# Graph attention kernel: VectorE adds the last step of a chunk in the next turn, behind the next chunk's scores, first messages and first product

## What is computed

```
Q = (h @ Wq).reshape(n, H, HD)
K = (h @ Wk).reshape(n, H, HD)
V = (h @ Wv).reshape(n, H, HD)
score = jnp.einsum('ehd,ehd->eh', K[src], Q[dst]) / np.sqrt(HD) + edge_bias
m = jax.ops.segment_max(score, dst, num_segments=n)
ex = jnp.exp(score - m[dst])
denom = jax.ops.segment_sum(ex, dst, num_segments=n)
attn = ex / denom[dst]
out = jax.ops.segment_sum(attn[:, :, None] * V[src], dst, num_segments=n)
```

## Time and profile before

| | us |
|---|---|
| median of 3 runs | 5411.74 |
| lowest and highest run | 5407.52, 5449.04 |
| span of the profiled execution | 5404.7 |
| first and last add of the pass (L785) | 309.2, 1864.1 |
| DVE busy over the whole span | 3064.0 (57%) |
| PE busy over the whole span | 3933.5 (73%) |

### The profile page before, as it was taken

The page is one execution under the profiler, slowest core; times in us unless marked ns, Lnnn a source line. Parts: engine busy times, 40 slices in busy tenths (PEclk is TensorE's granted clock), DMA queues, the critical chain, the costliest instruction groups (busy, mean ns, idle before and its releaser), DMA issues. The chain is left out here.

```text
span 5404.7 us, 69347 instructions
## 1 busy us (share of the span) xinstructions
PE 3933.5 (73%) x16281; PEld 2847.1 (53%) x16282; DVE 3064.0 (57%) x7623; ACT 1859.8 (34%) x5073; POOL 2464.9 (46%) x2442
## 2 busy tenths in 40 slices
PE   6867777777777659967853666666666338999999
PEld 4545555555555448856732444444444226777776
DVE  3278887878888766662154666666667773111111
ACT  1333333333333312311222444444444322333332
POOL 2256665656666450001166666666663422333332
PEclk8988988888888879977986788777887559999999
DMA  2555555555555232211173333333331451111111
GB/s 80 186 146 149 154 151 148 151 140 153 147 148 151 83 118 84 91 55 40 52 252 89 95 96 96 94 95 94 93 96 47 127 194 20 32 32 31 31 31 27
DMA packets 316127, 553.64 MB, mean 102 GB/s; under 512 B 63431, under 2 KB 213783, under 8 KB 315857
## 3 DMA queue, kind: packets, MB, share of 16 engines
q0 software_dynamic: 137120, 388.63, 27.4%
q1 hardware_dynamic: 178736, 161.98, 9.8%
HBM read 459.75 MB, written 90.62 MB: 102 GB/s over the span
## 5 line engine op out<-in xcount | busy, mean ns | idle before, releaser
L427 POOL DMA_INDIRECT attend_ring<-kv_rows,all_step_src x880 | 860.1, 977 | 624.5 <-PE attend_ps_agg L468 371.3
L931 POOL DMA_INDIRECT edge_ring<-head_rows,all_step_src x880 | 878.7, 999 | 457.1 <-issue 204.2
L967 PE MATMUL edge_ps_agg<-edge_msg,edge_sel 128*128 128x264 f32 x1760 | 676.3, 520 | 188.9 <-issue 57.3
L468 PE MATMUL attend_ps_agg<-attend_msg,attend_sel 128*128 128x264 f32 x1760 | 605.1, 445 | 179.7 <-DVE graph_qa L785 122.9
L967 PEld LDWEIGHTS edge_ps_agg<-edge_msg,edge_sel 128*128 128x128 f32 x1760 | 414.5, 257 | 328.2 <-issue 198.7
L1266 DVE TENSOR_TENSOR graph_acc<-graph_acc,edge_ps_agg 128x264 f32 x880 | 369.9, 420 | 367.2 <-PE edge_ps_agg L967 169.0
L2821 DVE TENSOR_TENSOR moe_gl<-moe_ps_h,moe_act 128x341 f32<-128x341 f32 x210 | 107.8, 514 | 776.8 <-PE moe_ps_h L2739 776.8
L452 PE MATMUL attend_ps_q<-graph_qa,attend_sel_t 128*128 x1760 | 527.7, 429 | 27.4 <-ACT attend_sel_t L581 17.8
L785 DVE SCALAR_TENSOR_TENSOR graph_qa<-graph_qa,all_step_same,attend_ps_agg 128x264 f32 x880 | 421.1, 479 | 170.1 <-remote 121.0
L468 PEld LDWEIGHTS attend_ps_agg<-attend_msg,attend_sel 128*128 128x128 f32 x1760 | 329.3, 208 | 347.2 <-issue 148.6
L2739 PE MATMUL moe_ps_h<-experts_w,moe_xt 128*128 x1680 | 501.7, 451 | 0.6 <-ACT moe_xt L2770 0.6
(11 more groups left out here) (424 smaller groups left out, 6587.9 us busy)
## 6 DMA issues: line engine op xcount, KB each, us to landing
attend_ring<-kv_rows,all_step_src POOLq DMA_INDIRECT x880
edge_ring<-head_rows,all_step_src POOLq DMA_INDIRECT x880
kv_rows<-qkv_kv SPq DMA_DIRECT2D x25, 512.0 KB, 2.9
experts_w<-in_w_t SPq DMA_DIRECT2D x16, 682.0 KB
attend_mask<-run_starts SPq DMA_DIRECT2D x440, 8.1 KB
edge_mask<-run_starts SPq DMA_DIRECT2D x440, 8.1 KB
head_rows<-hds_hh SPq DMA_DIRECT2D x25, 264.0 KB
qkv_x<-in_x SPq DMA_DIRECT2D x25, 256.0 KB, 3.3
```

What stands on the lines that cost most here:

```text
L427: nc.gpsimd.indirect_dma_start(ring[:, step % RING1, :], None, g.kv_rows, bass.IndirectOffsetOnAxis(g.step_src[:, step:step + 1], 0)).then ...
L468: nc.tensor.matmul(ps_agg[i % SUM_BANKS][:, 0:AGG], sel[:, q % 2, u % QU, :], msg[:, q % 2, u % QU, :], start=True, stop=True).then_inc(s_ ...
L931: nc.gpsimd.indirect_dma_start(ring[:, n % slots, u, :], None, g.head_rows, bass.IndirectOffsetOnAxis(g.step_src[:, step:step + 1], 0)).th ...
L967: nc.tensor.matmul(ps_agg[i % BANKS][:, 0:AGG], sel[:, q % 2, u % QU, :], msg[:, q % 2, u % QU, :], start=True, stop=True).then_inc(s_agg, 1)
```

## The change

The adds of a chunk's steps 0 to 14 stay where they are. The add of step 15 leaves the end of its turn. It now stands in the next turn behind score_of(a), messages(b, 0) and product(c, 0), and ahead of the load of the first eight block numbers (rows_of), which moves behind it with it. The rows of the last turn are handed on from turn to turn as last. Behind the last turn one add is left. No instruction is added or taken away.

```diff
-            def turn(c, a, b):
-                at = rows_of(b, 0) if b is not None else [None] * U
+            def turn(c, a, b, last):
                 of(a, score_of)
                 of(b, messages, 0)
                 of(c, product, 0)
+                if last is not None:
+                    add(b - 1, last, CH - 1)
+                at = rows_of(b, 0) if b is not None else [None] * U
                 of(a, tails_of)
                 of(c, product, 1)
                 of(a, heads_of)
...
                 of(b, add, at, 12)
                 of(b, add, at, 13)
                 of(c, dot, 3)
-                of(b, add, at, 14, 15)
-
-            turn(0, None, None)
-            turn(1, 0, None)
+                of(b, add, at, 14)
+                return at if b is not None else None
+
+            last = turn(0, None, None, None)
+            last = turn(1, 0, None, last)
             for i in range(1, count - 1):
-                turn(i + 1, i, i - 1)
-            turn(None, count - 1, count - 2)
-            turn(None, None, count - 1)
+                last = turn(i + 1, i, i - 1, last)
+            last = turn(None, count - 1, count - 2, last)
+            last = turn(None, None, count - 1, last)
+            add(count - 1, last, CH - 1)
             v.wait_ge(s_add, count * CH)
```

## The result

The changed kernel takes 5491.68 us (median of 4 runs, 5483.99 to 5497.41), the kernel before 5423.92 us beside it (4 runs, 5407.52 to 5449.04). The ratio is 1.0135, with a 95% interval of 1.0111 to 1.0158: 1.35% slower, clear of noise. The prediction's direction was wrong. The prediction said 5407 us, in a range of 5370 to 5438. The profiled execution of after has a span of 5482.0 us, 77.3 more than before.

The account below looks back on a forecast made before the run. A chain of hand-overs, with add-up 15's late signal, then ACT and PE, was taken to set the turn. Span 5404.7 less 5 gave 5399.7; plus 7.0 to the runs' median, 5407 us, range 5370 to 5438.

Parts of the forecast that it names:

- (a): At the turn's end, DVE's score, messages and product fill idle time ahead of add 15, cutting it from 121 to 47 us.
- (c): After add 15, DVE could start scan L700 0.75 us behind it and reach copy L710 about 1.4 us earlier.
- the wait at L710: DVE's wait at copy L710 for PE's row product was to grow from 50.7 to some 125 us.
- (d): Queue behind copy L710 gains nothing: PE waits for ACT, ACT for add-up 15's signal, which hangs on PE alone.
- R2: Rival: add-up 15's signal comes earlier because PE's transpose is queued sooner; all of it 121 us, 5291 us; chance 0.04.
- (e): New waits: add 15 ends up to 1.1 us later where its signal is prompt, hidden by ACT's 2.2 us.
- (f): At copy L710, 14 turns where DVE is late gain 0.33 us each, 5 us in all.
- R3: Rival: PE's clock drops behind the idle stretch after add-up 15, 1.57 us per turn, 83 us, 5495 us; chance 0.07.
- The sign that it named: For the clock loss on PE: the granted clock of the first graph's pass falls below 0.88.
- R1: Rival: DVE's lead counts in full, each turn 1.4 us shorter, 74 us, 5338 us; chance 0.08.

Follow-up runs that it names:

- e5: Changed kernel with ACT's first denominators of the next chunk ahead of its wait for add-up 15: 0.9993 of before (5414.85 us), again 0.9977 (5409.26 us), on late chips.
- e1: Changed kernel with DVE's score back behind add 15, first messages and product still ahead: 1.0034 of before on a calm chip, repeats 1.0040, 1.0042 and 1.0031.
- e2: Changed kernel with only the score ahead of add 15, first messages and product behind it again: 1.0043 of before on a calm chip, repeats 1.0037 and 1.0033.
- e6: Kernel before with ACT's first denominators of the next chunk ahead of its wait for add-up 15: 1.0062 of before, 5451.85 us, on a late chip.
- e7: Changed kernel with PE's transpose of the scores issued six times instead of once: 1.0138 of before on a late chip.
- e8: Changed kernel with PE's transpose issued six times and add-up 2 of each chunk four times: 1.0169 of before on a late chip.
- e9: Changed kernel with first-pass gathers cut to 64 of 512 values per row, ring zeroed first, for timing only: 5075.44 us, 1.009 of before, on a calm chip.

## Why the prediction was wrong, step by step

- (a) held as to the work: DVE does it from 1062.29 to 1063.77, in idle time. It did not hold as to the idle time. 116.9 us are left, 47 were expected: the signal moved away by nearly as much as was filled.
- (c) and the wait at L710 held: 119.3 us, some 125 expected. On a calm chip 39.8 became 95.6.
- (d) failed. Its sentence was "G itself hangs on PE alone". The engine that makes the signal did nothing later, and still the signal came 1.15 us later on average, 3.06 instead of 1.91 behind the shown end; that is two thirds of the 1.74 us that a turn lost. The rest of (d), that DVE's lead leads nowhere because the copy waits for PE and PE for ACT, held: PE's first add-up kept its 2.16 us behind ACT, and when e5 takes ACT away, messages that are there early let it start 4.7 us sooner, for 1.5 us of the turn. The prediction noted that it did not know what holds the signal, and priced that only in the direction of a gain (R2).
- (d) was also short of a term: PE reaches its waits for DVE earlier and works at a lower clock behind them. Between the copy and the carries that is 0.27 of the 0.37 us that a turn loses on a calm chip. Over the pass the adds run over 1422.1 us there, against 1406.8 in before, 15 of the 22 us by which the medians differ.
- (e) held as to what follows ACT: PE's first add-up started 2.16 us behind it, 2.17 before.
- (f), the gain of 5 us in turns where DVE is late at the copy, is not to be seen on either kind of chip.
- R3 gave 5495 us, close to the 5491.68 measured, by luck: its reason, the clock behind the idle stretch, carries a third of the loss or less (0.51 of 1.74 us per turn). The sign that it named came, the granted clock of the pass fell from 0.88 to 0.86, but nearly half of the loss in clock (0.37 of 0.80 us per turn, each stretch weighted by what its clock lacks to full) lies between add-up 15 and PE's next add-up, where PE has next to no work. ACT to PE's first add-up took as long as before, and the stretch that R3 priced at 1.57 us more per turn cost 0.21.
- R1 and R2 fell. R1 was right about what it would need: that PE does not wait for ACT.

What lengthens the lag stays open. Over seven traces of late chips it is 1.91 and 2.52 us with DVE's old order, and 3.06 to 3.39 us with the new one, in which the transpose is queued early and DVE works on while the signal is out. The new order brings both at once, the halves that would part them (e1, e2) met only calm chips, and e6 shows that something else moves it too. In after the lag is over 2.6 us in 45 of 51 turns, before in 6. That one late chip's signals are late and a calm chip's are not, with the same program, is likewise not explained; both gather rows back to back at that point of the turn.

The traces hold three marks that a next test should start from; none of them is a cause shown. First, the lag comes in levels: in before it is 1.2 to 1.9 us in 34 of 51 turns, in after 2.6 to 3.3 us in 30 and more in 15. Second, within a level it goes with POOL's gathers. Where POOL's next gather starts over 0.6 us behind the add-up's shown end, the lower level is 1.68 us (31 turns of before) and the upper 3.07 (28 of after). Where it starts at 0.3 to 0.5 us, they are 1.32 (3 turns) and 2.79 (2), and 2.64 to 2.87 in nine such turns of e7 and e8. Third, the late chips' traces hold 41,000 to 42,300 records of semaphore updates and the calm chips' 73,200 to 73,800, at nearly the same number of instructions; records of PE, DVE and ACT and of the DMA landings are missing alike. So what sets the two kinds of chip apart is not in PE's signals alone. That the gathers hold the signal was to be tested by e9, which met a calm chip, and is untested.

## What to carry to other kernels

Idle time in front of an instruction is not free room if nobody can say what ends it: before filling it, find the engine whose lateness sets the turn. And test moves together as well as alone: here, on late chips, the line of ACT alone cost 0.6%, the DVE order alone 1.35%, and both together came out level with the kernel before (0.9993) and 0.2% below it (0.9977). And when one engine arrives earlier only to wait for PE, it can cost: here PE then stood still longer in front of its own next wait, and was slower behind it.

## What the hardware showed that I had not expected

- The same program took 5031 to 5033 us in five batches and 5418 to 5424 us in three, 7.7% apart. In this pass it is the late signal and a lower clock behind it: 28.74 against 25.91 us per turn, 1.87 of it the lag and 0.98 the stretch to the copy. The second graph's pass has the same mark. The group of its add, on the first chip and then on a calm one:

```profile
L1266 DVE TENSOR_TENSOR graph_acc<-graph_acc,edge_ps_agg 128x264 f32 x880 | 369.9, 420 | 367.2 <-PE edge_ps_agg L967 169.0 <-remote 165.3 <-issue 18.9
```

```profile
L1266 DVE TENSOR_TENSOR graph_acc<-graph_acc,edge_ps_agg 128x264 f32 x880 | 366.0, 416 | 31.1 <-PE edge_ps_agg L967 19.4 <-DVE graph_acc L1266 2.0 <-issue 0.9
```

- The lag of one matmul's signal ran from 0.04 to 4.6 us within one execution of after, and its mean changed with the order of other engines' instructions.
- Throwing work at an idle PE raised its clock from 0.55 to 1.00 in the stretch behind, and most of what that gained was lost later in the same turn, at a granted clock of 0.94 there instead of 0.98.
